# A four-layer graph network: the gate network moved into the pass that sorts the edges

## What is computed

```python
gate = jax.nn.silu(edge_attr @ W1.T + b1) @ W2.T + b2
gate = gate + adapt_logit
cw = jnp.where(distances < CUTOFF, 0.5 * (jnp.cos(jnp.pi * distances / CUTOFF) + 1.0), 0.0)
mj = node_mult[dst]
msg = gate * h[dst] * (cw * mj)[:, None]
agg = jax.ops.segment_sum(msg, src, num_segments=N)
tot = jax.ops.segment_sum(mj, src, num_segments=N)
```

## Time and profile before

| what | us |
|---|---|
| median of three executions | 19301.86 (19296.92 to 19310.93) |
| profiled execution, its own time | 19300.93 |
| its span, first to last instruction | 19299.1 |
| setup and counting | about 0 to 468 |
| record pass | about 468 to 4476 |
| gate pass | about 4491 to 5897 |
| second layer's messages | about 8343 to 9860 |

### The profile page before, as it was taken

The page is one execution under the profiler, slowest core; times in us unless marked ns, Lnnn a source line. Parts: engine busy times, 40 slices in busy tenths (PEclk is TensorE's granted clock), DMA queues, the critical chain, the costliest instruction groups (busy, mean ns, idle before and its releaser), DMA issues. The chain is left out here.

```text
span 19299.1 us, 464781 instructions
## 1 busy us (share of the span) xinstructions
PE 12159.3 (63%) x134887; PEld 10568.7 (55%) x134888; DVE 14400.3 (75%) x31210; ACT 5527.5 (29%) x13966; POOL 7447.6 (39%) x7744
## 2 busy tenths in 40 slices
PE   5666666667884565657756465566556656666666
PEld 4666666666662555544545455455545555555555
DVE  8666666664442897789978998899867786786776
ACT  0111111114662552034420352055104203402410
POOL 0777777774333003633310004600550270073055
PEclk7555555558996887678888556755776786776677
DMA  6333333334553999979977687788759977976986
GB/s 257 105 105 105 104 105 105 104 104 147 168 165 64 325 345 354 390 282 331 315 217 244 233 296 251 225 297 296 236 162 408 330 236 292 388 236 233 406 276 186
DMA packets 2220132, 4547.89 MB, mean 236 GB/s; under 512 B 718350, under 2 KB 1002604, under 8 KB 2219270
## 3 DMA queue, kind: packets, MB, share of 16 engines
q1 hardware_dynamic: 1232502, 2012.08, 32.6%
q0 software_dynamic: 437168, 1287.73, 21.1%
q10 hardware_dynamic: 550368, 1246.92, 17.4%
HBM read 2775.60 MB, written 1814.28 MB: 238 GB/s over the span
## 5 line engine op out<-in xcount | busy, mean ns | idle before, releaser
L1397 POOL DMA_INDIRECT sum_slots<-messages,sum_rows x2820 | 2665.7, 945 | 6657.2 <-ACT sum_rows L1409 5800.2
L1480 PE MATMUL sum_sums<-sum_slots,sum_onehot 128*128 128x144 bf16 (+1 forms) x31584 | 3042.9, 265 | 2054.3 <-DMA sum_slots<-messages,sum_rows 800.8
L1480 PEld LDWEIGHTS sum_sums<-sum_slots,sum_onehot 128*128 128x128 bf16 x31584 | 2662.5, 116 | 2434.7 <-issue 2434.7
L696 POOL DMA_INDIRECT records<-rec,row_i x3125 | 3035.2, 971 | 1430.8 <-issue 929.3
L1200 PE MATMUL exp_rows<-tab,h 128*128 x40608 | 1971.2, 216 | 1446.6 <-DVE h L1233 1439.6
L1200 PEld LDWEIGHTS exp_rows<-tab,h 128*128 128x128 bf16 x40608 | 1814.6, 115 | 1603.4 <-issue 1560.2
L666 PE MATMUL ps_l<-place,turned 98*128 98x98 f32 x6250 | 1391.6, 402 | 1258.5 <-ACT place L576 1256.7
L1206 PE MATMUL exp_rows<-tab,h 128*128 x13536 | 1489.0, 288 | 836.9 <-ACT exp_stage L1335 682.0
L666 PEld LDWEIGHTS ps_l<-place,turned 98*128 98x128 f32 x6250 | 1262.5, 303 | 1371.6 <-issue 1371.4
L1206 PEld LDWEIGHTS exp_rows<-tab,h 128*128 128x128 bf16 x13536 | 1278.0, 128 | 1047.6 <-issue 1038.2
L1409 ACT COPY sum_rows<-idx_g 128x2 int32 (+1 forms) x1692 | 322.2, 192 | 4008.6 <-DMA sum_slots<-messages,sum_rows 3200.8
(11 more groups left out here) (287 smaller groups left out, 21958.0 us busy)
## 6 DMA issues: line engine op xcount, KB each, us to landing
exp_places<-src_places SPq DMA_DIRECT2D x1692, 512.0 KB, 6.0
messages<-exp_stage ACTq DMA_DIRECT2D x1410, 576.0 KB, 11.2
messages_first<-exp_stage ACTq DMA_DIRECT2D x282, 832.0 KB, 5.6
sum_slots<-messages_back SPq DMA_DIRECT2D x282, 600.0 KB, 4.3
messages_back<-fill ACTq DMA_DIRECT2D x624, 270.5 KB
l_places<-dst_places SPq DMA_DIRECT2D x282, 512.0 KB, 6.1
gates<-gate SPq DMA_DIRECT2D x282, 408.0 KB, 2.6
l_gate<-gates SPq DMA_DIRECT2D x282, 408.0 KB
```

The costliest lines, as they stand in the source:

```text
L696: pool.indirect_dma_start(rec_dram, bass.IndirectOffsetOnAxis(ap=row_i[:, g, k:k + 1], axis=0), rec[:, g, k, :], None).then_inc(put[g], 16)
L1397: pool.indirect_dma_start(gath[:, c, g, :], None, of_dram, bass.IndirectOffsetOnAxis(ap=row_g[:, c, g:g + 1], axis=0)).then_inc(g_dma[c], 16)
L1480: last = pe.matmul(sums[:, c % RS, g, 0:3 * width], onehot[:, c % RS, g * B + k, :], of[:, k * 3 * width:(k + 1) * 3 * width], start=(k == ...
```

## The change

- Records have 56 numbers: 48 gates and 8 fields. The field DWIN goes and ONE (a constant 1) comes, so that the second layer finds one, MASK and CW behind the gates, as before.
- The gate network runs in the record pass, on the edges in input order: five edges per partition at a time, attributes in a tile `attr_in` of their own. `rec` now gets gates times CW from DVE. POOL waits for the gates instead of the load. The look-up's PSUM (`ps_l`) and `turned` have three buffers for five groups, beside one buffer each of `ps_a`, `ps_h` and `ps_g`.
- The gate pass keeps `fields`, `shifts` and the scatters; PE has no program there. Nothing is stored; the tensor `gates` is gone, and the second layer reads the records instead.
- The zeros for `records` and `src_places_and_weights` are queued on SP in the first block, behind the small loads, in place of the second.

```diff
-EW, MASK, CW, DREL, DREL3, SREL, SWIN, DWIN = range(8)
+ONE, MASK, CW, EW, DREL, DREL3, SREL, SWIN = range(8)
-    REC = R + NF
+    REC = D + NF
@@ first block, SP, behind the small loads (from the second block) @@
+                    for dram, per in ((rec_dram, NS * REC), (sent_dram, NS * 2)):
+                        view = dram.rearrange("(p n) f -> p (n f)", p=P)
+                        many, rest = per // FZ, per % FZ
+                        with sp.Fori(0, many) as n:
+                            sp.dma_start(view[:, bass.ds(n * FZ, FZ)], fill[:, :]).then_inc(s_fill, 16)
...
@@ record pass @@
+        bank = (0, 1, 2, 0, 1)
-                            lone_wait(sp, put[g], i * (16 * K))
-                        sp.dma_start(rec[:, g, :, 0:R], attr[:, bass.ds((i * R5 + g) * K, K), :]).then_inc(ld[g], 16)
+                            lone_wait(sp, s_at, i * R5 + (g + 1 - R5))
+                        sp.dma_start(attr_in[:, g, :, :], attr[:, bass.ds((i * R5 + g) * K, K), :]).then_inc(ld[g], 16)
@@ ACT @@
+                    def attributes(i, first, g):
+                        act.wait_ge(s_at, i * R5 + (g + 1))
+                        if g or not first:
+                            act.wait_ge(s_hidden, i * R5 + g)
+                        act.copy(attr_t[:, :], ps_a[0:2 * R, 0:KP * P]).then_inc(s_attr, 1)
+                    def silu(i, first, g):
+                        act.wait_ge(s_hidden, i * R5 + (g + 1))
+                        if g or not first:
+                            act.wait_ge(s_g, i * R5 + g)
+                        act.activation(act1[0:2 * D, :], ps_h[0:2 * D, 0:KP * P], ACT.Silu,
+                                       bias=b1_col[:, :], scale=1.0).then_inc(s_silu, 1)
                     def turn(i, first):
...
-                            act.copy(turned[0:W, g, :], ps_t[0:W, 0:K * P]).then_inc(s_copy, 1)
+                            act.copy(turned[0:W, bank[g], :], ps_t[0:W, 0:K * P]).then_inc(s_copy, 1)
+                            attributes(i, first, g)
+                            if g:
+                                silu(i, first, g - 1)
+                            elif not first:
+                                silu(i - 1, False, R5 - 1)
@@ DVE, before onehots(i, False, g) @@
+                    def gated(i, first, g):
+                        n = i * R5 + (g + 1)
+                        dve.wait_ge(s_g, n)
+                        dve.wait_ge(s_meta, n)
+                        dve.tensor_tensor(
+                            rec[:, g, :, 0:D], ps_g[:, 0:K * D].rearrange("p (k f) -> p k f", k=K),
+                            emeta[:, bass.ds((i * R5 + g) * K, K), CW].unsqueeze(2).to_broadcast([P, K, D]),
+                            ALU.mult).then_inc(s_gate, 1)
+                            if g >= 3:
+                                gated(i, False, g - 3)
+                            else:
+                                gated(i - 1, False, g - 3 + R5)
@@ PE @@
+                    def turn_attributes(i, first, g):
+                        lone_wait(pe, ld[g], i * 16 + 16)
+                        if g or not first:
+                            lone_wait(pe, s_attr, i * R5 + g)
+                        for q in range(KP):
...
+                    def hidden(i, first, g):
+                        pe.wait_ge(s_attr, i * R5 + (g + 1))
+                        if g or not first:
+                            lone_wait(pe, s_silu, i * R5 + g)
+                        pe.matmul(ps_h[0:2 * D, 0:KP * P], w1t[:, :], attr_t[:, :],
+                                  start=True, stop=True).then_inc(s_hidden, 1)
+                    def gates(i, first, g):
+                        pe.wait_ge(s_silu, i * R5 + (g + 1))
+                        if g or not first:
+                            lone_wait(pe, s_gate, i * R5 + g)
+                        for q in range(KP):
...
+                            if g:
+                                hidden(i, False, g - 1)
...
+                            if g >= 2:
+                                gates(i, False, g - 2)
...
                             if g:
                                 look(i, False, g - 1)
...
                             turn_windows(i, False, g)
+                            turn_attributes(i, False, g)
@@ POOL @@
-                            lone_wait(pool, ld[g], i * 16 + 16)
+                            lone_wait(pool, s_gate, i * R5 + (g + 1))
@@ gate pass: transposes, hidden, gates, attrs, silu, gated and store are removed @@
@@ second layer @@
-                            sp.dma_start(gate[:, q, :, :],
-                                         gate_view[:, bass.ds(i * (RG * B) + c * CS, CS), :]).then_inc(ldg[q], 16)
+                            sp.dma_start(gate[:, q, :, :].rearrange("p (g k) f -> p g (k f)", k=B),
+                                         slot_rows[:, bass.ds(i * RG + c * CH, CH), :]).then_inc(ldg[q], 16)
```

More of the change, by code:

```diff
@@ L222, in gnn_kernel @@
             NWT = ceil_div(EC, P)
+            FILLS = []
             with nc.Block() as block:
@@ L303, in _ @@
                         sp.dma_start(w2t[2 * D:2 * D + 1, k * D:(k + 1) * D], row(b2)).then_inc(s_in, 16)
+                    for dram, per in ((rec_dram, NS * REC), (sent_dram, NS * 2)):
[3 more added lines that the diff above has]
+                            sp.dma_start(view[:, bass.ds(n * FZ, FZ)], fill[:, :]).then_inc(s_fill, 16)
+                        if rest:
+                            sp.dma_start(view[:, many * FZ:per], fill[:, 0:rest]).then_inc(s_fill, 16)
+                        FILLS.append(16 * (many + (rest > 0)))
                 @block.gpsimd
@@ L394, in _ @@
                 def _(sp):
[L396 to L403, removed]
                     for t in range(NWT):
@@ L526, in gnn_kernel @@
                                          "update", "product", "rank"))
+            s_one, s_at, s_attr, s_hidden, s_silu, s_g, s_gate = (
+                sem(f"s1_{n}") for n in ("ones", "attributes_turned", "attributes", "hidden", "silu", "gates", "gated"))
             attr = edge_attr.rearrange("(p n) f -> p n f", p=P)
@@ L653, in look @@
                         n = i * R5 + (g + 1)
-                        at = lambda k: ps_l[:, g, k * W:(k + 1) * W]
+                        at = lambda k: ps_l[:, bank[g], k * W:(k + 1) * W]
                         pe.wait_ge(s_same, n)
-                        if not first:
-                            pe.wait_ge(s_mul, i * R5 + (g + 1 - R5))
+                        ago = next(d for d in range(1, R5 + 1) if bank[(g - d) % R5] == bank[g])
+                        if g >= ago or not first:
+                            pe.wait_ge(s_mul, i * R5 + (g + 1 - ago))
                         for k in range(K):
@@ L665, in look @@
                         for k in range(K):
-                            last = pe.matmul(at(k), turned[0:W, g, k * P:(k + 1) * P], place[0:W, :],
+                            last = pe.matmul(at(k), turned[0:W, bank[g], k * P:(k + 1) * P], place[0:W, :],
                                              start=False, stop=True, skip_group_check=True)
@@ new lines, in hidden @@
+                    def hidden(i, first, g):
[9 more added lines that the diff above has]
+                        for q in range(KP):
+                            m = min(2, K - 2 * q) * D
+                            last = pe.matmul(ps_g[:, q * 2 * D:q * 2 * D + m],
+                                             act1[:, q * P:(q + 1) * P], w2t[:, 0:m], start=True, stop=True)
+                        last.then_inc(s_g, 1)
@@ L810, in turn @@
-                    def turn(i, first):
-                        for t in range(RH):
-                            if t % 2 == 0:
-                                fields(i, first, t // 2)
-                            attrs(i, first, t)
-                            if t:
-                                silu(i, first, t - 1)
-                            elif not first:
-                                silu(i - 1, False, RH - 1)
-                    act.wait_ge(s_one, 1)
-                    turns(act, TURNS, turn)
@@ L868, in _ @@
+                            last = act.copy(to[:, at, :, :].rearrange("p g k b -> p (g k) b"),
+                                            recc[:, c, :, D + n].unsqueeze(2).to_broadcast([P, CS, 2]))
+                        last.then_inc(s_meta, 1)
+                    def turn(i, first):
+                        for c in range(RC):
+                            fields(i, first, c)
+                    turns(act, TURNS, turn)
                 @block.vector
```

192 lines of the change are left out of this document (63 added, 129 removed).

## The result

The changed kernel takes 19465 us (median of eight executions, 19355 to 19530) beside 19299 us for the kernel before on the same chip: a ratio of 1.0079, with a 95% interval of 1.0054 to 1.0103. The profiled execution took 19529.8 us. The forecast was 19167 us and faster; what came is rival (a), priced at 19542. The executions of the kernel before lie within 24 us of each other, those of the changed one within 175.

The account below looks back on a forecast made before the run. Bounds were taken as POOL in the record pass, PE in the gate pass, DVE in the counting and second layer. 19300.9 + 247 + 294 - 685 + 10 = 19167 us; range 18870 to 19690.

Parts of the forecast that it names:

- rival (a): Record pass: PE falls behind, its clock granted at 0.70; 7.45 us per group, +669 instead of +294, 19542 us; chance 0.30.
- Part 1, +247: First block: the moved zero stores on SP's queue hold all engines at the block's end, costing 247 us.
- Part 2, +294: Record pass: added gate network makes PE's chain decide; 6.85 us per group against POOL's 6.38, costing 294 us.
- The two ends of a group: Record pass: PE's chain per group takes 8.9 us at the low clock and 5.6 at the high one.
- I take 0.80, between the first two: Record pass: PE's granted clock assumed 0.80, between counting's 0.78 and second layer's 0.87, so 40% of the time low.
- the prediction's own formula: Record pass: mean group length if the ring evens out fast and slow, 1 / (0.6/5.6 + 0.4/8.9) = 6.58 us.
- the prediction's own sign: Record pass: the forecast counts as wrong if the period lies outside 6.6 to 7.1 us.
- Rival (b): Record pass: added work keeps PE's clock high, POOL stays the bound at 6.38 us per group, 18873 us; chance 0.12.
- the sentence cited in the prediction: PE's clock: the skill says the default is throttled and activity releases it, which by itself would give 18873 us.
- Part 3, -685: Gate pass: without its network, POOL's two scatters per chunk bound it; 1406 us becomes 721, gaining 685.
- Part 4, +10: Second layer: reading 448 KB per chunk in place of 408 costs 10 us, between 0 and 36.

Follow-up runs that it names:

- the other orders with idle products and late zeros: Changed kernel with ScalarE's and PE's record-pass orders changed, four unread products before each hidden product, zero stores back in the second block: 18641 us, ratio 0.9657.
- silu early with late zeros: Changed kernel with ScalarE's silu moved ahead of `turned` and the attribute copy, and the zero stores back in the second block: 18685 us, ratio 0.9673.
- a shorter chain: Changed kernel with silu, attribute copy, then `turned` on ScalarE, and attributes turned ahead of windows on PE: 19066 us, ratio 0.9876.

## Why the prediction was wrong

**Part 1, +247: right.** The first `turned` copy starts 248.4 us later than before (718.5, 470.1), and the experiments give 276, 267 and 240. What decided was not the transfers but in which block SP's queue was held by them. The Trainium skill's sentence on issuers ("DMA: Bandwidth & Descriptors", Issuing engines are not separate DMA queues), that transfers of all issuers run on the same 16 engines, is neither borne out nor contradicted by this: no run here gives the stores to another issuer.

**Part 2, +294: the step that failed.** From the first to the last `turned` copy it is 4605.0 us in place of 3972.1, +633. The two ends of a group were right, 8.83 and 5.47 us measured for 8.9 and 5.6, and so was what PE waits for. What failed is the sentence "I take 0.80, between the first two": the clock was taken from the means of other stages, as if the amount of work on PE set it. It was 0.68, and half of the groups ran low. Put into the prediction's own formula, 0.68 is 64% of the time low and gives 1 / (0.36/5.6 + 0.64/8.9) = 7.34 us, for 7.38 measured; so the clock was the term that failed, and POOL's pace, which the forecast mixed in with 6.38, held few groups. By the prediction's own sign, a period outside 6.6 to 7.1 us, the forecast was wrong. Rival (a) had the reason, "the rest of 1.8 us in each group stands in every cycle", and the price; it should have been weighed above the forecast, for the one row that told of short, regular rests, 0.56 with 1.89 us per group, was this stage's own. That the rests are the cause is shown by filling them (-521 us) and by shortening the longest (-502 us), with the clock at 1.00 and 0.99. Rival (b) had the price of a pass at POOL's pace, 18873, beside 18906 and 18925 in these two kernels.
The Trainium skill ("TensorE: Matmul & The Clock Gate", A second HAM failure mode: psum-queue depth-cycling) tells of a kernel in which TensorE idles briefly between groups of products and the clock goes back and forth; this trace agrees, with 313 of 624 group lengths at the low level and falls after rests of 1.35 us. By the sentence cited in the prediction, that activity releases the throttle, the clock would have been high here. It was high in the kernels with the rests filled or shortened; in the changed kernel it fell although PE rested for only 1.35 us in groups of 5.47.

**Part 3, -685: nearly right.** The copies of L865 take 719.7 us from first to last, those of L791 before 1395.0: -675. The pitch of 1.27 us and the bound by POOL were as forecast.

**Part 4, +10: right in size**, +2.6 us (1503.3 us from the first to the last `l_scaled`, 1500.7 before). Some 23 us more lie in stages that the change doesn't touch. From the gate pass's last copy to the end, the profiled executions with the changed gate pass on these chips differ by 36 us among themselves (13402 to 13438; 13412 before), so no cause is read out of it.

**The sum.** 248 + 633 - 3 (between the two passes) - 675 + 3 + 23 = 229 us, the difference of the spans. With +633 in place of +294 the forecast becomes 19506, for 19530 in that execution. The range, 18870 to 19690, held the time; the forecast inside it had the wrong sign. The spread of the executions goes with the clock too: the mean granted clock of a whole execution is 0.710 in the shortest of the eight and 0.698 in the longest. But it isn't all in this pass: the two profiled executions of the changed kernel differ by 91 us, 57 of them in the record pass (7.38 and 7.29 us per group) and 34 behind the gate pass, where no cause was looked for. Every kernel with silu ahead or with idle products spreads by 8 to 18 us, in four or five executions each; two of them have a clock of 0.71, so it is not a high clock alone that steadies them.

What beats both: the other orders with idle products and late zeros, 18641 us (ratio 0.9657, 0.9641 to 0.9673), and without idle work, silu early with late zeros, 18685 us (0.9673, 0.9660 to 0.9686).

## What to carry to other kernels

Moving work from a stage bound by TensorE into one bound by something else is worth what was forecast for it only if TensorE keeps its clock there; look for its short, regular rests in the new stage before adding up its work, and take the clock from a row with like rests and not from a row with like work. Work that TensorE waits for is best done first on the engine that does it: here one moved silu gave 502 us. And a store that hides behind a block's work keeps its cover only as long as it stays in that block, for at the end of a block all engines wait for the slowest queue.

## What was not expected of the hardware

- Idle products on TensorE, 0.55 us per group at the full clock, made a kernel 2.7% faster, by a clock of 1.00 in place of 0.69.
- The two ways of a group, 5.47 and 8.83 us, alternate in stretches with nothing else changed; a shorter chain (4.5 and 7.9) did not end it, rests of 0.92 and 1.17 us in place of 1.35 and 0.72 did.
- On one chip the same instructions took as long as elsewhere, but a waiting engine started up to 1.52 us after the end of what it waited for (0.13 at most on another), and the kernel before took 21533 us. With most scatters left out, the hand-over took 0.04 us there too and the record pass was as on the other chips, 7.37 us per group, so in these runs the late starts went with the scatters. What delays the hand-over there stays open.
